# Side work of TensorE in a scan row: kv blocks, attention and projection issued at other states of a decoder kernel

## Chip, core and metric

One core of a Trainium2 chip. The metric is the device time of one execution in microseconds (us), as the median of several runs. The kernel before has a median of 1000.1 us of 3 runs (999.48 to 1000.89). All arithmetic is in f32.

## What is computed

A decoder layer on `x` of shape (4, 512, 512) with a context of shape (4, 512, 256). It has three stages, each with a residual and a normalization. The last stage (a feed-forward net whose weights are read from a table of 16 values by index) is not touched by the change.

```python
x = layernorm(x + attention(x, weight_qkv, weight_proj))      # 16 heads of 32, 4 kv heads, over the 4 positions
x = layernorm(x + ssm(ctx_1024, x, ...))                      # x is the gate
x = layernorm(x + ffn(x, lut, gate_idx, up_idx, down_idx))

# attention: seq is axis 0 of x (4 positions), batch is axis 1 (512)
scores = einsum("bhqd,bhkd->bhqk", q, k) / sqrt(32)           # causal over 4 positions
out = softmax(scores) @ v @ weight_proj.T

# ssm, for each of the 4 rows b of the context:
x  = einsum("ed,bld->bel", in_proj_w, hidden)                 # 512 channels, 512 steps
u  = silu(causal_conv(x, conv_w) + conv_b)
dt_lo, B, C = split(einsum("ke,bel->bkl", x_proj_w, u))       # 16, 16, 16
delta = softplus(dt_proj_w @ dt_lo + dt_proj_b)
state[n] = state[n] * exp(delta * A[n]) + delta * u * B[n]    # 16 states n, scan over the 512 steps
y = sum_n state[n] * C[n] + D * u
y = y * silu(z)
```

## The kernel before

**The scan.** The ssm is worked off in four rows b (0 to 3), one for each row of the context. A row has 16 states n, and a state has four units et, one for each block of 128 channels. A unit is one scan on VectorE over 512 steps (`scan`, line 1166). Before it TensorE transposes the scaled input of the unit into one of four PSUM banks (`input_transposed`, line 630, "input transposes" below), for which ScalarE has made `scaled` (line 865), and ScalarE makes the decay of the unit (line 876, a ring of eight). After the scan GpSimd multiplies the state with the repeated row of C (line 1414). When a state's four units are done, GpSimd issues a DMA that adds the whole state into `y_scratch` in DRAM (`add_group`, line 1425, 1 MB); the buffer of the state is free again when that has landed. There are four such buffers, so the scan of state n waits for the addition of state n-4 (`group_sum`). States with an odd n are added into a second tensor, and one DMA per row adds this to the first (`add_odd_sum`, line 1432, at state 4 of the next row). The last eight states of row 3 are summed on TensorE instead (`state_summed`, line 639).

**Order.** TensorE transposes for unit k once the scan of unit k-4 is done, so it runs at most four units ahead of VectorE. Every engine works in order. There is no planner: the tables that begin at line 174 say after which unit (n, et) of a row a job is issued, and the functions of each engine are written to agree with them.

**Side jobs.** While row b is scanned, TensorE also does the attention of position block b (`attention_transposed`, "att" i for positions i = 3, 0, 2, 1, line 583), its projection (`project`, line 592), and for the next row: the input projection (`in_proj`, line 519), x_proj (line 542), the kv blocks (`project_kv`, "kv" s, four of them, line 528), the transposes of B and u (lines 549, 561), dt (`delta_mm`, line 555), q (line 534), and the transposes of delta (line 568). These jobs use PSUM banks 4 to 7 in rotation, by their place in `ORDERED` (`BANK`): a job waits until the job four places before it has been read out (`freed`, `bank_freed`). Two of the places belong to "expneg", on which TensorE does nothing and which only takes a bank for ScalarE.

**Who reads them.** ScalarE copies att (`keep_attT`, line 845), kv (`keep_kv`, line 789), B and C (`keep_bc`, line 799), and does the first half of softplus (`softplus_parts`, lines 811 to 820), each at the end of a state n of its loop, behind the scaled inputs and the decays for state n+2. VectorE does the second half (`softplus`, lines 1128, 1131, 1133, 1138) after the units (9,0) and (11,0), and the head products of q after (11,2), (11,3) and (12,1). Its third step, line 1133, is the last to read the bank of dt (`base_ready`). VectorE adds the projection to x (`residual`, line 1153) and takes its statistics; GpSimd makes the normalization factors (`norm_factors`, lines 1437 to 1445), and ScalarE applies them (`normalized`, line 853).

**GpSimd in a row** does the four products of each state, ten products of the attention's weights with v in states 0 to 3 (`weighted_values`, line 1403), and issues the additions: that of state n after the product of unit (n+1, 1).

**Row 3** has no next row, so its attention, projection, residual and normalization come early in the row (`LAST_ATT_AT`, `LAST_PROJ_AT`, `LAST_RES_AT`). SP loads the finished rows 0 to 2 (`load_row`, lines 418 and 420, 768 KB and 1 MB) at states 8 to 10, each after the repeated C row of its state has been issued, which waits for the products of the state before.

## Time and profile before

| | |
|---|---|
| median of 3 runs | 1000.1 us |
| the profiled execution | 997.59 us, of it 995.8 us from the first to the last instruction |
| the scan of rows 0 to 3 | from 54.4 to 551.1 us of the span |
| TensorE, share of the span busy | 87% (864.1 us) |
| VectorE | 76% (757.6 us) |
| ScalarE | 68% (674.1 us) |
| GpSimd | 50% (495.0 us) |
| granted TensorE clock, mean | 0.909 of 2.4 GHz |

Times in the profile are microseconds from the start of the span, if not marked ns. PE is TensorE, PEld its weight loads, DVE VectorE, ACT ScalarE, POOL GpSimd, SP SyncE. L630 is line 630 of the kernel. A line of a timeline has the start, the duration, the engine, the line and the operation, how many were merged (x4), and in brackets the idle time of the engine before it and what ended that. The granted clock is a share of 2.4 GHz: 1.00 is 2.4 GHz and 0.50 is 1.2 GHz. The shares of the whole span say little about the scan, in which each stretch has another engine or the DMA that ends last; the waits and the timelines tell that.

### The profile page before, as it was taken

The page shows a single profiled execution, that of the slowest core. Times are in us where ns is not written, and L with a number is a line of the kernel's source. Part 1 is how long each engine was busy: PE and PEld are TensorE (multiplying, and loading weights), DVE is VectorE, ACT ScalarE, POOL GpSimd, SP SyncE. Part 2 cuts the span into 40 slices and gives each one's busy share as a digit, 9 for nine tenths or more (in the row PEclk, how much of TensorE's full clock was granted, in tenths as well). Part 3 has the DMA queues.
Part 4 walks back from the last instruction along what each step waited for, and adds up shares of the span by engine and source line. Part 5 has one row for each costly group of instructions (what it writes and reads, how often), then busy time and mean ns, then how long its engine had stood idle before and what let it go on. Part 6 is the DMA issues. An engine that isn't in the chain of part 4 may idle for free.

```text
span 995.8 us, 11868 instructions
## 1 busy us (share of the span) xinstructions
PE 864.1 (87%) x3824; PEld 624.7 (63%) x3824; DVE 757.6 (76%) x1053; ACT 674.1 (68%) x994; POOL 495.0 (50%) x458
## 2 busy tenths in 40 slices
PE   6879887797779778788878988899999999899997
PEld 3447544476445565446544566787777778688885
DVE  3797898875898859987678776888888888345542
ACT  4698985788956898659598365767777776242321
POOL 0079867897857979569999731122211221001000
PEclk9889788897679796997878989999999999999999
DMA  8167989589976799977999022111111110223211
GB/s 263 34 178 171 203 182 210 134 222 239 211 197 139 201 223 234 226 146 166 220 255 324 36 96 85 43 43 56 49 42 42 42 63 21 74 85 99 93 64 53
DMA packets 49907, 135.98 MB, mean 137 GB/s; under 512 B 5364, under 2 KB 13684, under 8 KB 41156
## 3 DMA queue, kind: packets, MB, share of 16 engines
q0 software_dynamic: 8064, 58.72, 30.5%
q1 hardware_dynamic: 40432, 76.44, 22.6%
q10 hardware_dynamic: 1364, 0.25, 0.2%
q8 instruction: 23, 0.38, 0.1%
q14 instruction: 24, 0.20, 0.1%
HBM read 57.93 MB, written 81.66 MB: 140 GB/s over the span
## 4 chain that ended last, share of the span: by engine, by line
PE 22%; issue 22%; DVE 14%; POOL 13%; DMA 9%; ACT 3%; DVEq 1%; ACTq 0%; POOLq 0%
DMA y_scratch<-state 9%; POOL state L1414 7%; PE banks L703 5%; PE banks L727 4%; PE banks L592 4%; DVE leaf L1194 3%; DVE w_gu L1194 3%; PE banks L630 3%; PE banks L639 3%; ACT leaf L984 2%; DVE state L1166 2%; PE banks L534 2%; POOL prod_a L1403 2%; POOL y_scratch L1425 1%; DVE idx_sb L1178 1%
## 5 line engine op out<-in xcount | busy, mean ns | idle before, releaser
L1414 POOL TENSOR_TENSOR state<-state,crep 128x512 f32<-128x512 f32 x256 | 350.7, 1658 | 67.5 <-DVE state L1166 67.5
L1166 DVE TENSOR_TENSOR_SCAN state<-decay,banks 128x512 f32<-128x512 f32 x256 | 296.5, 1204 | 73.8 <-PE banks L630 47.0
L703 PE MATMUL banks<-x2T,wgu 128*128 128x512 f32 x1056 | 246.5, 393 | 5.4 <-DVE hT L1244 4.0
L630 PE MATMUL banks<-ident,scaled 128*128 128x128 f32 x1024 | 175.5, 316 | 79.4 <-DVE state L1166 69.2
L630 PEld LDWEIGHTS banks<-ident,scaled 128*128 128x128 f32 x1024 | 138.2, 162 | 153.5 <-DVE state L1166 67.6
L703 PEld LDWEIGHTS banks<-x2T,wgu 128*128 128x128 f32 x1056 | 197.9, 189 | 52.9 <-DVE hT L1244 11.4
L876 ACT ACTIVATE decay<-delta,negA 128x512 f32<-128x512 f32 x256 | 171.0, 718 | 85.0 <-DVE state L1166 84.6
L865 ACT ACTIVATE scaled<-duT,BT 128x512 f32<-128x512 f32 x256 | 163.4, 716 | 0.0
L984 ACT ACTIVATE leaf<-idx_sb,table,table_gap 128x1024 f32<-128x1024 uint8 (+1 forms) x132 | 129.4, 1022 | 6.8 <-DVE w_down L1194 3.2
L1194 DVE COPY_PREDICATED leaf<-idx_sb,leaf 128x1024 f32<-128x1024 uint8 (+1 forms) x88 | 94.5, 1073 | 6.3 <-issue 5.5
L1497 POOL TENSOR_TENSOR pool_wait_here<-minus_half 128x1 f32<-128x1 f32 x22 | 4.3, 194 | 180.0 <-DVE w_gu L1194 115.4
L727 PE MATMUL banks<-x2T 128*128 128x512 f32 (+1 forms) x264 | 83.0, 396 | 3.5 <-DVE x2T L1353 3.5
L727 PE MATMUL banks<-x2T,wgu 128*128 128x512 f32 (+1 forms) x264 | 81.5, 390 | 0.0
L1537 POOL TENSOR_TENSOR rstd<-vareps,minus_half 128x1 f32<-128x1 f32 x16 | 8.7, 542 | 140.6 <-DVE vareps L1372 140.6
L1425 POOL DMA_DIRECT2D y_scratch<-state x52 | 59.2, 1139 | 14.4 <-DMA y_scratch<-state 14.4
L592 PE MATMUL banks<-wp,attT 128*128 128x512 f32 x128 | 61.4, 625 | 0.0
L727 PEld LDWEIGHTS banks<-x2T 128*128 128x128 f32 (+1 forms) x264 | 50.6, 192 | 14.6 <-issue 3.9
L727 PEld LDWEIGHTS banks<-x2T,wgu 128*128 128x128 f32 (+1 forms) x264 | 49.6, 188 | 10.4
L1194 DVE COPY_PREDICATED w_gu<-idx_sb,leaf 128x1024 f32<-128x1024 uint8 x33 | 53.3, 1615 | 3.0 <-issue 2.7
L1065 ACT ACTIVATE leaf<-leaf,shift,rstd 128x512 f32<-128x512 f32 x16 | 13.1, 816 | 62.6 <-DVE shift L1375 62.6
L534 PE MATMUL banks<-wqkv,xT_sb 128*128 128x512 f32 x96 | 47.7, 646 | 3.7 <-DVE conv_in L1133 3.7
L1077 DVE SCALAR_TENSOR_TENSOR conv_in<-banks,ch,conv_in 128x511 f32<-128x511 f32 (+2 forms) x48 | 35.4, 744 | 11.9 <-ACT conv_in L773 10.7
(137 smaller groups left out, 1125.0 us busy)
## 6 DMA issues: line engine op xcount, KB each, us to landing
y_scratch<-state POOLq DMA_DIRECT2D x52, 1024.0 KB, 8.8
crep<-c_scratch SPq DMA_DIRECT2D x64, 256.0 KB, 5.7
idx_sb<-in_idx SPq DMA_DIRECT2D x11, 512.0 KB, 3.5
xT_sb<-in_xT SPq DMA_DIRECT2D x16, 256.0 KB, 4.5
y_scratch<-u SPq DMA_DIRECT2D x4, 1024.0 KB, 6.0
y_scratch<-state SPq DMA_DIRECT2D x4, 1024.0 KB, 6.3
y_scratch<-y_scratch POOLq DMA_DIRECT2D x4, 1024.0 KB, 12.8
leaf<-x_scratch SPq DMA_DIRECT2D x16, 256.0 KB, 2.8
```

What stands on the lines that cost most here:

```text
L534: last = mm(banks[:, bank, :], xT_sb[:, t, s, :], wqkv[:, t, 0:QT * P], start=t == 0, stop=t == HT - 1)
L592: last = mm(banks[:, bank, :], attT[:, s, t if s else 0, :], wp[:, t, :], start=t == 0, stop=t == QT - 1)
L630: last = nc.tensor.transpose(banks[:, k % NB, lc * LQ:(lc + 1) * LQ], scaled[:, g % SR, lc, et * P:(et + 1) * P], ident[:])
L703: last = mm(banks[:, 2 * tb + w, :], wgu[par][:, w, ws, t * P:(t + 1) * P], x2T[:, tb, xs, t, :], start=t == 0 and n == 0, stop=t == HT - ...
L727: last = mm(banks[:, bank, :], h[0:rows], w[0:rows, f, :], start=f == 0 and n == 0, stop=f == FT - 1 and n == 2)
L865: A(scaled[:, g % SR, lc, :], duT[m % 2][:, lc, :], ACT.Copy, scale=BT[:, m % 2, lc, n:n + 1])\
L876: A(decay[:, k % DR_RING, :], delta[m % 2][:, et, :], ACT.Exp, scale=negA[:, et, n:n + 1])\
L984: A(buffer(LEAF_ROLE[j], kind, parity), bit_of(0, kind, parity), ACT.Identity, bias=table[:, 2 * j:2 * j + 1], scale=table_gap[:, j:j + 1] ...
L1166: V.tensor_tensor_scan(state[:, g % GR, et, :], decay[:, k % DR_RING, :], banks[:, k % NB, :], 0.0, ALU.mult, ALU.add).then_inc(scan_ready, 1)
L1194: V.copy_predicated(buffer(kept, kind, parity), bit_of(bit, kind, parity), buffer(other, kind, parity)).then_inc(mux_ready, 1)
L1414: G.tensor_tensor(state[:, g % GR, et, :], state[:, g % GR, et, :], crep[:, g % CR, :], ALU.mult)\
L1425: pool.dma_start(total[:, b], group(g), accum_op=ALU.add).then_inc(group_sum(g)[0], 16)
```

## The change

In rows 0 to 2, attention 2 is issued after unit (3,2) instead of (4,1), kv 0 and 1 after (5,0) and (5,2) instead of (4,2) and (4,3), kv 2 and 3 after (9,1) and (9,2) instead of (6,0) and (6,1). ScalarE's copies of them move to match: attention 2 from state 4 to 3, kv 0 and 1 from 4 to 5, kv 2 and 3 from 5 to 9, ahead of the softplus parts. As banks go by the order of jobs, the jobs that a job waits for change too.

In row 3, the four attention jobs, the four projections, the residual adds, the normalization and the copies go to later units, the row loads on SP from states 8 to 10 to states 9 to 11, and the loads of the lookup table and of the first indices from state 11 to 12.

```diff
-                   (4, 2): ("kv", 0), (4, 3): ("kv", 1), (6, 0): ("kv", 2), (6, 1): ("kv", 3),
+                   (5, 0): ("kv", 0), (5, 2): ("kv", 1), (9, 1): ("kv", 2), (9, 2): ("kv", 3),
...
-        ATT_AT = {(3, 0): 3, (3, 1): 0, (4, 1): 2, (6, 0): 1}
-        LAST_ATT_AT = {(3, 0): 3, (3, 1): 0, (4, 0): 2, (5, 0): 1}
+        ATT_AT = {(3, 0): 3, (3, 1): 0, (3, 2): 2, (6, 0): 1}
+        LAST_ATT_AT = {(3, 2): 3, (3, 3): 0, (4, 2): 2, (6, 0): 1}
...
-        LAST_PROJ_AT = {(5, 1): 3, (5, 3): 2, (6, 1): 1, (6, 3): 0}
+        LAST_PROJ_AT = {(6, 2): 3, (7, 0): 2, (7, 2): 1, (8, 0): 0}
...
-                        if b == S - 1 and n == 8:
+                        if b == S - 1 and n == 9:
                             sp.wait_ge(shift_ready, S)
                             sp.wait_ge(x1_out, 16 * (S - 1))
-                        if b == S - 1 and 8 <= n < 8 + S - 1:
-                            load_row(n - 8)
-                        if b == S - 1 and n == 11:
+                        if b == S - 1 and 9 <= n < 9 + S - 1:
+                            load_row(n - 9)
+                        if b == S - 1 and n == 12:
                             sp.dma_start(table[:], lut.to_broadcast([P, 16])).then_inc(lut_in, 16)
...
-                        if n == 2:
+                        if n == (2 if more else 3):
                             keep_attT(b, 3)
                             keep_attT(b, 0)
-                        elif n == (4 if more else 3):
+                        elif n == (3 if more else 4):
                             keep_attT(b, 2)
-                        elif n == (5 if more else 4):
+                        elif n == 5:
                             keep_attT(b, 1)
-                        if n == 8 and not more:
+                        if n == 9 and not more:
                             normalized(b)
...
                             elif n == 4:
                                 keep_bc(m)
+                            elif n == 5:
                                 keep_kv(c, 0)
                                 keep_kv(c, 1)
-                            elif n == 5:
-                                keep_kv(c, 2)
-                                keep_kv(c, 3)
                                 keep_bt(m)
...
                             elif n == 9:
+                                keep_kv(c, 2)
+                                keep_kv(c, 3)
                                 softplus_parts(m, (2, 3))
...
-                LAST_RES_AT = {(5, 2): 3, (6, 0): 2, (6, 2): 1, (7, 0): 0}
+                LAST_RES_AT = {(6, 3): 3, (7, 1): 2, (7, 3): 1, (8, 1): 0}
...
-                            if at == ((15, 2) if more else (7, 1)):
+                            if at == ((15, 2) if more else (8, 2)):
                                 norm_factors(b)
```

## Rows read from the trace of the kernel before

**Rows 1.** Waits of VectorE, 205 to 249 us: total us, times, longest.

```profile
DVE state L1166 <- PE banks L630: 8.4, 6, 3.1
```

**Rows 2.** Timeline of VectorE, rows 0 and 1: start, us, operation, idle before.

```profile
116.43 1.29 DVE L1128 TENSOR_SCALAR delta<-banks 128x512 f32<-128x512 f32 x2
...
237.25 4.55 DVE L1166 TENSOR_TENSOR_SCAN state<-decay,banks 128x512 f32<-128x512 f32 x4 [5.53 <-DMA y_scratch<-state]
...
251.92 1.28 DVE L1133 SCALAR_TENSOR_TENSOR conv_in<-banks,conv_in 128x512 f32<-128x512 f32 x2
...
254.31 8.99 DVE L1166 TENSOR_TENSOR_SCAN state<-decay,banks 128x512 f32<-128x512 f32 x8
```

**Rows 3.** Chain that ended last, row 1: start, us, what.

```profile
219.22 18.01 DMA y_scratch<-state
...
237.75 10.63 DMA y_scratch<-state
```

**Rows 4.** Stretches: length, busy PE, PEld, DVE, ACT, POOL; clock, DMA share, GB/s.

```profile
79.00:119.00 40.00, 34.62 (x202) 26.71 (x200) 30.48 (x30) 39.94 (x71) 39.17 (x34) 0.91 0.88 182
187.00:219.00 32.00, 23.36 (x141) 17.99 (x140) 26.83 (x28) 28.72 (x46) 32.00 (x30) 0.89 0.79 203
219.00:249.00 30.00, 24.02 (x136) 18.89 (x136) 19.03 (x17) 27.18 (x50) 24.29 (x23) 0.83 1.01 232
```

**Rows 5.** Waits of ScalarE, 79 to 118 us (row 0).

```profile
ACT decay L876 <- DVE state L1166: 0.4, 1, 0.4
```

**Rows 6.** Timeline of ScalarE, row 0: copies of kv 2 and 3, Ln.

```profile
101.40 0.67 ACT L789 ACTIVATE kv<-banks 128x256 f32<-128x256 f32 x2
...
115.80 1.09 ACT L820 ACTIVATE conv_in<-banks 128x512 f32<-128x512 f32 x2
```

**Rows 7.** Timeline of VectorE, row 3: states 7 and 11 to 15.

```profile
498.96 1.22 DVE L1166 TENSOR_TENSOR_SCAN state<-decay,banks 128x512 f32<-128x512 f32 x1 [1.59 <-DMA y_scratch<-state]
...
526.30 24.80 DVE L1166 TENSOR_TENSOR_SCAN state<-decay,banks 128x512 f32<-128x512 f32 x20 [6.95 <-DMA y_scratch<-state]
```

**Rows 8.** Timeline of GpSimd, row 3: normalization factors and the addition of state 7.

```profile
506.24 0.23 POOL L1437 TENSOR_SCALAR vareps<-meanvar 128x4 f32<-128x4 f32 x1
...
508.16 4.96 POOL L1414 TENSOR_TENSOR state<-state,crep 128x512 f32<-128x512 f32 x4
513.08 0.91 POOL L1425 DMA_DIRECT2D y_scratch<-state  x1
```

**Rows 9.** Chain that ended last, row 3.

```profile
513.08 13.20 DMA y_scratch<-state
```

**Rows 10.** DMA issues of the page: count, KB each, median us to landing.

```profile
y_scratch<-state POOLq DMA_DIRECT2D x52, 1024.0 KB, 8.8
```

**Rows 11.** Timeline of TensorE, row 1: a kv block, input transposes, dt 2.

```profile
224.31 1.89 PE L528 MATMUL banks<-wqkv,xT_sb 128*128 128x256 f32 x8
226.04 0.60 PE L630 MATMUL banks<-ident,scaled 128*128 128x128 f32 x4
...
252.65 2.07 PE L555 MATMUL banks<-bc_dt,dt_w 17*128 17x512 f32 x2 [2.10 <-DVE conv_in L1133]
```

**Rows 12.** Stretches again, columns as in rows 4.

```profile
252.10:262.20 10.10, 8.70 (x25) 5.29 (x26) 10.10 (x12) 9.11 (x17) 8.53 (x8) 0.50 1.04 229
...
525.20:531.90 6.70, 4.23 (x11) 2.67 (x12) 5.59 (x6) 3.76 (x6) 5.33 (x5) 0.50 1.03 407
```

**Rows 13.** Timeline of TensorE: q 3 of rows 0 and 1, q 2 of row 2.

```profile
133.24 5.05 PE L534 MATMUL banks<-wqkv,xT_sb 128*128 128x512 f32 x8 [0.31 <-DVE conv_in L1133]
...
266.32 6.76 PE L534 MATMUL banks<-wqkv,xT_sb 128*128 128x512 f32 x8 [1.70 <-DVE conv_in L1133]
...
403.71 3.60 PE L534 MATMUL banks<-wqkv,xT_sb 128*128 128x512 f32 x8
```

**Rows 14.** Timeline of SP, row 3: first row load.

```profile
511.12 0.42 SPq L418 DMA_DIRECT2D rows_in<-x_scratch  x1
```

**Rows 15.** Timeline of TensorE, row 3: input transposes of (12,0).

```profile
527.67 1.09 PE L630 MATMUL banks<-ident,scaled 128*128 128x128 f32 x4 [6.13 <-DVE state L1166]
```

## Prediction, made before the changed kernel was run

> **What bounds the kernel now.** I read the views in this order: who waited for whom on VectorE, the busy time of the engines by stretch, the chain that ended last, and then the timelines around each moved job. The scan takes 64 groups of four units ("state n of row b" below is one group; "(n, et)" is one unit); the change touches nothing outside it. The question for each moved job is whether TensorE is what ends last where it stands, and where it will stand.
>
> Row 1 stands for rows 1 and 2, which repeat each other. In its states 3 to 8 VectorE waits 8.4 us for the input transposes [rows 1], because attention, x_proj and the kv blocks stand before them in TensorE's queue. The reader is to see that a second wait comes behind these: the scan of state 7 starts at 237.25 after 5.53 us without work, released by a DMA [rows 2]. That DMA is the addition of state 3, issued at 219.22 and landed 18.01 us later [rows 3]. GpSimd issues it, and GpSimd is busy for 32.00 of the 32 us before that [rows 4]: ten attention products and four state products per state, with no wait for a scan. From 219 to 249 the 16 DMA engines are busy all the time (share 1.01), by the addition, the sum of the odd states and the repeated C rows [rows 4]. So here a faster TensorE moves neither the issue nor the landing. The next addition follows in the same chain (237.75, 10.63 us) [rows 3], and it releases state 9. After that VectorE has no gap up to the q jobs: softplus and scans are back to back [rows 2].
>
> Row 0 has no sum of a row before it, and additions land in time. But ScalarE is busy for 39.94 of the 40 us from 79 to 119 [rows 4], with one wait of 0.4 us [rows 5]: silu, decays, scaled inputs, evictions, softplus parts. Its last Ln starts at 115.80 [rows 6] and softplus on VectorE at 116.43 [rows 2], so ScalarE is what ends last there.
>
> In row 3 GpSimd and the DMA bound the first half as in row 1. The end is set by one wait: the scan of state 11 starts at 526.30 after 6.95 us of waiting [rows 7] for the addition of state 7, which GpSimd issued at 513.08 [rows 8] and which took 13.20 us [rows 9], where the median of 52 such additions is 8.8 [rows 10].
>
> **The change, part by part.** *States 3 to 6, rows 0 to 2.* Attention 2 goes from (4,1) to (3,2), kv 0 and 1 from (4,2), (4,3) to (5,0), (5,2), kv 2 and 3 from (6,0), (6,1) to (9,1), (9,2). The TensorE waits there (7.7 of the 8.4 us; the rest are in state 8) shrink to some 4 us. In rows 1 and 2 this is worth nothing: the cover is GpSimd's queue and the 18.01 us landing, and they don't move. In row 0 ScalarE is the cover, and the one thing taken from its queue before the softplus is the pair of evictions of kv 2 and 3, 0.67 us as a pair with an overlap of about 0.1 [rows 6]: -0.6 us. ScalarE's other evictions only change places, each behind a decay that waits for the scan of the same state, so the matmul it waits for is done by then: nothing.
>
> *kv 2 and 3 in state 9.* This is the term that costs. The banks of side jobs rotate over four, by the order of jobs. In the new order kv 2 takes the bank of dt 0 and kv 3 that of dt 1, which are free only when the third step of softplus (L1133) has read them. That step stands in VectorE's queue behind the scan (9,0) and starts at 251.92 [rows 2]; today dt 2 waits for the same thing and starts at 252.65 [rows 11]. So kv 2 starts at 252.65 with the transposes of (9,2), (9,3) and of state 10 queued behind it, which today are done at 249. VectorE gets to (9,1) at 254.31 [rows 2] and would want (9,2) at 255.45 and (9,3) at 256.58. TensorE has to do kv 2 (1.89 us as a span, 1.73 without its drain), transposes (0.44 of its 0.60), kv 3, transposes [rows 11]: 2 x 2.17 = 4.34 us at the full clock, ready at 256.99: 0.4 late. But the clock is granted at 0.50 (1.2 GHz) from 252.1 to 262.2 [rows 12], and dt 2 runs 2.07 us in it [rows 11]; the wait before kv 2 will be longer than today's, so I take this level for its start. How much a dense run begun just after such a fall loses until 2.4 GHz is back is bounded by the q jobs: 5.05 us in row 0 and 6.76 in row 1 against 3.60 at the full clock [rows 13]: 1.45 to 3.16 us lost. So (9,3) comes 1.9 to 3.6 us late; the middle is 2.75 us. dt 2 and 3 behind it fit between the scans (a wait of 0.86 for each against 1.13 for a scan). Nothing between here and the row's end can take it back, since VectorE is on the path. Three rows: 3 x 2.75 = +8.25 us; bounds 3 x 0.4 (full clock all through) and 3 x 3.6.
>
> The Trainium skill (TensorE: Matmul & The Clock Gate, section "Why this matters for your kernels") speaks against this change: it asks for matmuls kept together, since gaps bring the slow clock back, while spreading makes gaps. The rows agree in kind (0.50 after each idle stretch). What it makes of the time is the rival of the half clock that holds, below.
>
> *q jobs.* They begin 3 us later, and the clock may be at another level then. Today q 3 is at half clock in part in rows 0 and 1 and at the full one in row 2 [rows 13]. Row 1 could gain up to the 3.2 us, row 2 could lose as much. I take 0, with 3 us to both sides.
>
> *Row 3.* Attention and projection go back by 2 to 6 units, the residual adds too (to (6,3), (7,1), (7,3), (8,1)), the normalization factors on GpSimd from (7,1) to (8,2), the row loads on SP from state 8 to 9, the lookup table and the indices from 11 to 12. Up to the scan of state 7 (498.96, released by a DMA [rows 7]) the jobs have slack of GpSimd's making. Then there are three effects. (1) The factors take GpSimd 506.24 to 508.16 ahead of the products that precede the addition of state 7 [rows 8]. Behind it, that issue moves from 513.08 to 511.1. (2) The first row load, 1.77 MB, is issued at 511.12 [rows 14] and shares the DMA engines with the addition. At state 9 SP first waits for the products of state 8 (about 517), so the addition runs nearly alone: between the median of 8.8 and its own 13.20 [rows 9, 10] I take 11.2, landed at 522.3. (3) Against it: two residual adds (3.1 us of VectorE) now stand in state 7 and one in state 8, where one stood. The scans of states 9 and 10 go back, and state 11 can start at 521.6 to 522.8. Both ends meet at about 522.6: 3.7 us ahead of 526.30. (4) TensorE stands idle for 6.13 us before the next transposes at 527.67 and runs them and the first state sums at 0.50 clock up to 531.9 [rows 12, 15]; with the gap gone, half of its 4.23 busy us in that stretch, 2.1 us, can go too; I take 1.5. ScalarE's normalization now waits for the factors until 516 and ends at 519, ahead of the decays of state 12 that are wanted at 525. GpSimd's products, back to back at 4.9 us a state from 517, end at 552, before TensorE's last sum at 555.5: no new bound. The last row load moves only if the odd sum does, and is wanted 3 us later than it comes. Sum: -5.2 us; bounds -1.5 and -6.2.
>
> For the shared DMA engines the Trainium skill (Trainium Kernel Development and Optimization, section "Key Constraints") says that DMAs from SP, ScalarE and GpSimd run on the same 16 engines and interleave. The trace agrees: 13.20 against 8.8 us. If the queues were apart, effect (2) would be nothing and the gain of row 3 some 3 us.
>
> Sum: -0.6 + 8.25 - 5.2 = **+2.4 us**. It is made against the profiled execution (span 995.8, its own time 997.59) and put on the median of 1000.1, which lies 2.5 us above that execution and more than 1 us above no run shown: 1002.5.
>
> **The rivals.**
> *The clock comes back early (faster).* If TensorE is at 2.4 GHz when kv 2 starts, or is so within a microsecond, the cost is 0.4 to 1 us a row, and with row 3 at -5.8 the sum is -0.6 + 1.5 - 5.8 = -4.9: 995.2. It turns at 1.7 us a row. For it: row 1's clock is 1.00 just before 252, and today's run there is not dense. Against: both q runs, and the idle stretch before kv 2 grows.
> *Row 3 gives nothing.* The row load only meets the addition at another moment, or VectorE's later residuals set state 11: +7.6, less 1.5: 1006 to 1008.
> *The half clock holds.* 3.6 us in all three rows, +10.8 - 0.6 - 5.2 = +5.0: 1005.
> *The TensorE waits were the bound.* Then 3 x 4 us go and row 3's too: about -14, 986. Against it speaks the release of state 7 by a DMA in rows 1 to 3.
> *The change does not take effect*: excluded for the order of jobs; all tables are read by all engines.
>
> **How the numbers follow.** Forecast (0 to +5 us) 0.52, early clock 0.18, row 3 gives nothing 0.14, half clock holds 0.11, TensorE the bound 0.05. The range takes in the early clock's -4 and row 3's loss up to +7: 996.0 to 1007.0. What measurement can tell from no change is 0.2%, 2 us. The forecast's case lies around that bound: of its 0.52, 0.25 fall within and 0.27 above. Faster 0.22 (0.17 early clock, 0.05 TensorE the bound), within 0.2% 0.27, slower 0.51 (0.27 + 0.13 + 0.11).
>
> **What would show it.** State 7 of rows 1 and 2 should start as long after the first scan of its row as now, with a longer wait for the DMA; TensorE's kv 2 should start with L1133 of VectorE as its releaser; VectorE should have new waits for transposes at (9,2), (9,3), 2 to 3.6 us a row; state 0 of row 3 should start 5 to 10 us late; the addition of state 7 in row 3 should take under 12 us and the wait before state 11 shrink to about nothing. The prediction is wrong if state 9 shows no wait (clock at 1.00), or if row 3 from state 0 to the last sum isn't 4 to 6 us shorter.

## The result and the profile after

| | before | after |
|---|---|---|
| median, runs | 1000.07 us, 6 | 1008.25 us, 6 |
| lowest to highest | 999.48 to 1002.00 | 1005.09 to 1009.93 |
| the profiled execution | 997.59 us, span 995.8 | 1006.42 us, span 1004.6 |

The ratio is 1.0084 (95% interval 1.0067 to 1.0102): 8.2 us slower, where +2.4 was forecast, and above the range. First where the profiled execution became longer. The times are those of scans and of GpSimd's products, read from the timelines of both traces.

| stretch of the span | before | after | difference |
|---|---|---|---|
| start to the first scan | 54.43 | 55.45 | +1.0 |
| row 0, first scan to first scan of the next row | 127.50 | 128.69 | +1.2 |
| row 1 | 133.96 | 136.04 | +2.1 |
| row 2 | 130.03 | 136.44 | +6.4 |
| row 3, first scan to end of the last scan | 105.19 | 98.84 | -6.4 |
| row 3, first scan to end of TensorE's last state sum (L639) | 115.09 | 108.74 | -6.4 |
| row 3, first scan to end of GpSimd's last product (L1414) | 107.16 | 105.68 | -1.5 |
| GpSimd's last product to the end of the span | 442.70 | 442.27 | -0.4 |

In these two executions rows 0 to 2 cost 9.7 us; by the other traces of this study it is 7.3 to 9.3 (worked out under "Why the prediction was wrong"). Row 3 gave the scans and TensorE's sums even more than forecast (6.4 for 5.2). But the span became shorter by 1.5 + 0.4 there: it followed GpSimd, not TensorE. 1.0 + 9.7 - 1.5 - 0.4 = 8.8.

**Rows 0 to 2.** The timeline of VectorE after, row 0 and then row 1, answers [rows 2]:

```profile
116.89 1.29 DVE L1128 TENSOR_SCALAR delta<-banks 128x512 f32<-128x512 f32 x2 [1.52 <-ACT conv_in L820]
...
124.63 1.22 DVE L1166 TENSOR_TENSOR_SCAN state<-decay,banks 128x512 f32<-128x512 f32 x1 [1.74 <-PE banks L630]
126.79 3.44 DVE L1166 TENSOR_TENSOR_SCAN state<-decay,banks 128x512 f32<-128x512 f32 x3 [0.94 <-PE banks L630]
...
239.19 4.55 DVE L1166 TENSOR_TENSOR_SCAN state<-decay,banks 128x512 f32<-128x512 f32 x4 [10.18 <-DMA y_scratch<-state]
...
253.84 1.28 DVE L1133 SCALAR_TENSOR_TENSOR conv_in<-banks,conv_in 128x512 f32<-128x512 f32 x2
...
258.48 1.22 DVE L1166 TENSOR_TENSOR_SCAN state<-decay,banks 128x512 f32<-128x512 f32 x1 [1.04 <-PE banks L630]
260.64 3.44 DVE L1166 TENSOR_TENSOR_SCAN state<-decay,banks 128x512 f32<-128x512 f32 x3 [0.94 <-PE banks L630]
```

State 7 of row 1 starts 239.19 - 184.15 = 55.0 us after the row's first scan, where it was 55.3 (237.25 - 181.93), with 10.18 us of waiting for the DMA instead of 5.53: what TensorE gave back in states 3 to 6 went into that wait, and nothing else. In its place there are two new waits for TensorE at (9,2) and (9,3), 2.68, 1.98 and 2.14 us in rows 0, 1, 2. TensorE's side of them, with what ended its pause ([rows 11] show a kv block of 1.89 us):

```profile
120.02 3.78 PE L528 MATMUL banks<-wqkv,xT_sb 128*128 128x256 f32 x8 [5.66 <-DVE conv_in L1133]
...
254.57 3.43 PE L528 MATMUL banks<-wqkv,xT_sb 128*128 128x256 f32 x8 [4.27 <-DVE conv_in L1133]
...
258.27 1.89 PE L528 MATMUL banks<-wqkv,xT_sb 128*128 128x256 f32 x8
```

kv 2 waits for the third step of softplus, runs at 1.2 GHz after a pause of 4.3 to 5.7 us (granted clock 0.50 during it in row 0, 0.57 in row 1) and takes 3.4 to 3.8 us; kv 3 is at 2.4 GHz again (1.00 in row 1). This execution was a mild one. In kv23_only (below), and in the same way in four more traces with the pair in state 9, rows 1 and 2 lost more: kv 2 took 3.78 us and kv 3 still 2.1 to 2.7. Row 1 of kv23_only, where the granted clock was 0.50 during kv 2 and 0.77 during kv 3:

```profile
254.00 3.78 PE L528 MATMUL banks<-wqkv,xT_sb 128*128 128x256 f32 x8 [4.41 <-DVE conv_in L1133]
257.58 1.06 PE L630 MATMUL banks<-ident,scaled 128*128 128x128 f32 x4
258.43 2.46 PE L528 MATMUL banks<-wqkv,xT_sb 128*128 128x256 f32 x8
```

The waits of state 9 add up to 8.5 to 9.5 us over the three rows in these five traces, where the profiled execution of the changed kernel has 6.8.

**Row 3.** GpSimd's timeline answers [rows 8], and the DMA view of the microsecond of its issue (size, median us from issue to landing) answers [rows 9]:

```profile
520.99 1.46 POOL L1425 DMA_DIRECT2D y_scratch<-state  x1
522.09 1.67 POOL L1414 TENSOR_TENSOR state<-state,crep 128x512 f32<-128x512 f32 x1
523.85 0.23 POOL L1437 TENSOR_SCALAR vareps<-meanvar 128x4 f32<-128x4 f32 x1
```
```profile
y_scratch<-state POOLq DMA_DIRECT2D x1, 1024.0 KB, 10.0
```

The addition of state 7 is issued ahead of the factors and lands in 10.0 us instead of 13.20. VectorE's timeline then shows the 30 scans from (8,2) on in one piece, where [rows 7] had 6.95 us of waiting, and behind them the line that the forecast had not looked at:

```profile
520.79 34.68 DVE L1166 TENSOR_TENSOR_SCAN state<-decay,banks 128x512 f32<-128x512 f32 x30
555.39 6.96 DVE L1305 TENSOR_TENSOR table_gap<-table 128x8 f32<-128x8 f32 x1
562.38 0.17 DVE L1307 TENSOR_SCALAR table_gap<-table_gap 128x8 f32<-128x8 f32 x1
562.46 2.29 DVE L1210 TENSOR_TENSOR rows_in<-rows_in,gate_in 128x2048 f32<-128x2048 f32 x1
564.67 1.29 DVE L1173 TENSOR_SCALAR idx_sb<-idx_sb 128x1024 int32<-128x1024 int32 x2
...
573.30 4.42 DVE L1225 TENSOR_SCALAR vareps<-meanvar 128x2 f32<-128x2 f32 x1
```

A subtraction of 128x8 values lasts 6.96 us, and it ends with GpSimd's last product (562.31). In the kernel before it lasted 2.08 us and ended with that product too (553.08). VectorE there, and GpSimd's second gate product:

```profile
551.03 2.08 DVE L1305 TENSOR_TENSOR table_gap<-table 128x8 f32<-128x8 f32 x1
...
568.93 0.17 DVE L1225 TENSOR_SCALAR vareps<-meanvar 128x2 f32<-128x2 f32 x1
```
```profile
563.90 4.52 POOL L1481 TENSOR_TENSOR rows_in<-rows_in,gate_in 128x2048 f32<-128x2048 f32 x1
```

GpSimd after, from its last products on:

```profile
552.37 9.94 POOL L1414 TENSOR_TENSOR state<-state,crep 128x512 f32<-128x512 f32 x8
567.29 4.57 POOL L1481 TENSOR_TENSOR rows_in<-rows_in,gate_in 128x2048 f32<-128x2048 f32 x1 [4.98 <-issue]
...
573.16 4.53 POOL L1481 TENSOR_TENSOR rows_in<-rows_in,gate_in 128x2048 f32<-128x2048 f32 x1
577.79 1.74 POOL L1488 TENSOR_TENSOR rstd<-vareps,minus_half 128x2 f32<-128x2 f32 x1
```

So behind GpSimd's last product hangs a chain of fixed length: table_gap, a gate product on VectorE, the index bits (four in two pairs), two gate products on GpSimd, then the norm's power, which is queued behind them. Before, the second gate product ended at 568.42, 0.7 us before the norm's tensor_scalar, which comes by way of TensorE, was done (568.93 + 0.17); TensorE just set the end. After, the same tensor_scalar could start at 573.30, and the norm waits for GpSimd until 577.7.

### The profile page after: what moved, and what is told of

It is laid out like the page before. It is cut to its first block, busy times and chain, and to the rows that moved or that the text cites. A ratio compares the mean times of both kernels' runs of the same rounds, so it can differ in the third digit from the quotient of the medians.

```text
span 1004.6 us, 11868 instructions
## 1 busy us (share of the span) xinstructions
PE 861.9 (86%) x3824; PEld 623.5 (62%) x3824; DVE 765.5 (76%) x1053; ACT 674.7 (67%) x994; POOL 494.9 (49%) x458
## 4 chain that ended last, share of the span: by engine, by line
issue 19%; PE 16%; DVE 11%; ACT 3%; POOL 3%; DMA 2%; DVEq 0%; ACTq 0%; POOLq 0%
PE banks L703 5%; PE banks L727 4%; DVE leaf L1194 3%; PE banks L639 3%; DVE w_gu L1194 3%; DMA y_scratch<-state 2%; ACT leaf L984 2%; POOL state L1414 2%; PE banks L630 1%; PE banks L592 1%; DVE state L1166 1%; DVE idx_sb L1178 1%; DVE w_down L1194 1%; PE banks L676 1%; POOL rstd L1537 1%
## 5 line engine op out<-in xcount | busy, mean ns | idle before, releaser
L1414 POOL TENSOR_TENSOR state<-state,crep 128x512 f32<-128x512 f32 x256 | 351.9, 1700 | 75.9 <-DVE state L1166 75.8
L630 PE MATMUL banks<-ident,scaled 128*128 128x128 f32 x1024 | 168.6, 305 | 72.0 <-DVE state L1166 64.1
L630 PEld LDWEIGHTS banks<-ident,scaled 128*128 128x128 f32 x1024 | 131.4, 156 | 138.6 <-DVE state L1166 57.8
L1425 POOL DMA_DIRECT2D y_scratch<-state x52 | 62.8, 1207 | 14.4 <-DMA y_scratch<-state 14.4
L592 PE MATMUL banks<-wp,attT 128*128 128x512 f32 x128 | 66.5, 669 | 0.0
L1065 ACT ACTIVATE leaf<-leaf,shift,rstd 128x512 f32<-128x512 f32 x16 | 13.1, 816 | 62.6 <-DVE shift L1375 62.6
L528 PE MATMUL banks<-wqkv,xT_sb 128*128 128x256 f32 x128 | 37.0, 444 | 14.4 <-DVE conv_in L1133 14.4
```

The source lines that it names most:

```text
L592: last = mm(banks[:, bank, :], attT[:, s, t if s else 0, :], wp[:, t, :], start=t == 0, stop=t == QT - 1)
L630: last = nc.tensor.transpose(banks[:, k % NB, lc * LQ:(lc + 1) * LQ], scaled[:, g % SR, lc, et * P:(et + 1) * P], ident[:])
L1414: G.tensor_tensor(state[:, g % GR, et, :], state[:, g % GR, et, :], crep[:, g % CR, :], ALU.mult)\
L1425: pool.dma_start(total[:, b], group(g), accum_op=ALU.add).then_inc(group_sum(g)[0], 16)
```

## The experiments

The theories were made after the result was known. Theory A: the loss of rows 0 to 2 is all kv 2 and 3 in state 9. Theory C: the row-3 moves free TensorE by 6 us, but GpSimd's products set the end, so that they are worth 1 to 2 us. Theory B: the many gaps lower TensorE's clock everywhere.

**Parts of the change.** Four kernels. kv23_back is the changed kernel with:

```diff
-(9, 1): ("kv", 2), (9, 2): ("kv", 3)      # NEXT_AT
+(6, 0): ("kv", 2), (6, 1): ("kv", 3)
 # and keep_kv(c, 2), keep_kv(c, 3) in state 5 instead of 9
```

> The changed kernel with kv 2 and 3 put back after (6,0) and (6,1), their ScalarE copies in state 5; all else as changed. Theory A (kv 2 and 3 wait in state 9 for the banks of dt 0 and 1 and hold up the transposes; that is the whole loss of rows 0 to 2): no wait of VectorE for transposes in state 9, each row 0 to 2 some 2.5 us shorter than in the changed kernel, the total 7 to 10 us below it, at 998 to 1001. Theory B (the gaps that spreading makes keep TensorE at 1.2 GHz in more places, q and projection above all): half of the loss stays, 1003 to 1006.

kv23_only is the kernel before with only that pair moved, the other way:

```diff
-(6, 0): ("kv", 2), (6, 1): ("kv", 3)
+(9, 1): ("kv", 2), (9, 2): ("kv", 3)
```

> The kernel before with kv 2 and 3 alone moved to (9,1) and (9,2), copies in state 9. Theory A: slower than before by 6 to 10 us (rows 0 to 2 together 8 to 10 longer), 1006 to 1010. Theory B: only part of it, 1002 to 1005.

row3_only is the kernel before with LAST_ATT_AT, LAST_PROJ_AT, LAST_RES_AT, the factors, the loads and the evictions of row 3 as in the change; rows012_only is the changed kernel with all of these as before:

```diff
-LAST_PROJ_AT = {(5, 1): 3, (5, 3): 2, (6, 1): 1, (6, 3): 0}
+LAST_PROJ_AT = {(6, 2): 3, (7, 0): 2, (7, 2): 1, (8, 0): 0}
...
-if b == S - 1 and 8 <= n < 8 + S - 1:
+if b == S - 1 and 9 <= n < 9 + S - 1:
```

> The kernel before with the moves of row 3 alone (attention, projection, residual, normalization, row loads, table and index loads). Theory C (after the last scan the first VectorE operation with two SBUF inputs can't run until GpSimd has finished its last product, and the chain from there sets the end; TensorE's earlier end is worth nothing): scans of row 3 end 4 to 6 us earlier, GpSimd's last product 1 to 2 us earlier, the total 1 to 2 us below before, 998 to 999.5. The sum of the prediction (TensorE's last sum is the end): 5 us below, 995.

> The changed kernel with row 3 as before. Theory A with C: all of the loss and none of the 1 to 2 us of row 3: 1008 to 1011. By the prediction's sum for row 3: 1013.

Measured, beside runs of the kernel before on the same chip (median 999.51):

| kernel | median (lowest to highest) | ratio to before, 95% interval |
|---|---|---|
| kv23_back | 1000.03 (995.70 to 1001.91) | 1.0004 (0.9991 to 1.0016) |
| kv23_only | 1008.29 (1007.99 to 1011.34) | 1.0096 (1.0076 to 1.0116) |
| row3_only | 997.63 (994.22 to 999.99) | 0.9980 (0.9967 to 0.9993) |
| rows012_only | 1009.42 (1008.38 to 1010.55) | 1.0099 (1.0078 to 1.0121) |

Theory A holds within the intervals: the pair alone costs 9.6 us, and taking it back gives 8.0 (1.0084 - 1.0004). The row-3 moves are worth 2.0 us on the kernel before and 1.5 on the changed one (1.0099 - 1.0084), not 5.2: theory C. Theory B falls: with all moves but the pair in place the time is that of before. row3_only came 0.4 us under the 998 to 999.5 expected of it. The other moves of states 3 to 6 lie between +0.3 (rows012_only less kv23_only) and +2.4 us (kv23_back less row3_only), too near the intervals to tell. kv23_back isn't free of side effects: its row 0 took 77.3 us up to state 11, where the kernel before took 74.6, so the 8.0 is a less clean price of the pair than the 9.6.

The profiles of the four say which engine the end follows (us of each span, from the timelines):

| kernel | first scan to last scan's end, row 3 | last state sum to the end | GpSimd's last product to the end |
|---|---|---|---|
| before | 105.2 | 434.8 | 442.7 |
| kv23_only | 104.8 | 434.9 | 443.2 |
| rows012_only | 104.8 | 435.0 | 443.3 |
| after | 98.8 | 439.2 | 442.3 |
| kv23_back | 98.6 | 439.2 | 442.2 |
| row3_only | 98.8 | 439.1 | 442.1 |

From the first scan of row 3 to the end of the span it is 549.6 to 549.9 us in the three with row 3 as before, and 547.7 to 548.0 in the three with row 3 moved: 1.6 to 2.2 us, as the medians have it. (The execution of row3_only that was profiled was the slowest of its 11, 999.99 us; its row 3 is what is read here.)

With row 3 as before, TensorE's last sum and GpSimd's last product are both as far from the end as they can be, and neither has more than 1.2 us to spare. With row 3 moved, TensorE's sum comes 4.3 us earlier than the end can use, and the distance from GpSimd stays.

**The clock at kv 2.** Is it the clock that makes the two blocks cost 2 to 2.7 us a row, or their place behind the bank? The changed kernel, with matmuls of no use in the pause of TensorE (their output is overwritten):

```diff
 pe.wait_ge(*((scan_ready, k - NB + 1) if k >= NB else ramp_freed(k)))
+if g < DS * (S - 1) and g % DS == 9 and et == 1:
+    for _ in range(3):            # 5 in warm_kv5
+        mm(banks[:, k % NB, :], ident[:], wqkv[:, 0, 0:512], start=True, stop=True)
```

> Edit: the changed kernel, with three 128x512 matmuls of no use (into the bank that the next input transposes overwrite) ahead of the transposes of place (9,1) of rows 0 to 2, so that TensorE's matmuls come closer together before kv block 2. Clock theory (the kv blocks cost 2.0 to 2.7 us each row in state 9 because they run at 1.2 GHz): the clock is up when kv block 2 starts, the two blocks take half as long, the idle time of VectorE until TensorE in state 9 falls from 2.68, 1.98, 2.14 us to under 1 each, and the time comes to 1003 to 1006. Bank theory (the wait is the kv blocks' place in the ring of banks, at either clock): the waits of state 9 stay at 2 us or grow by the length of the added matmuls, and the time is 1008 to 1012.

> Edit: as warm_kv, with five idle-time matmuls instead of three. In warm_kv the pause of TensorE before kv block 2 was 4.22, 2.38 and 2.13 us in rows 0 to 2, the first kv block took 3.78, 2.54 and 1.99 us, and VectorE waited 2.88, 2.22 and 0.66 us in state 9: where the block was fast, the wait was short. Clock theory: the pauses are under 2.5 us in all rows, the kv block takes 2.0 to 2.6 us, the waits of state 9 are 0.4 to 1.2 us each and the time is 1000.5 to 1003. Rival (row 2 was chance, or the added matmuls delay the transposes of (9,1)): the waits stay at 2 us, the time is 1003 to 1007.

Measured: warm_kv 1003.16 us, ratio 1.0039 (1.0019 to 1.0059); warm_kv5 1003.28, ratio 1.0033 (1.0016 to 1.0049); the changed kernel had 1.0084. The execution of warm_kv that was profiled was the slowest of its 12, 1006.25 us, so its trace shows waits but not the gain. kv 2 on TensorE in warm_kv5, rows 0, 1 and 2:

```profile
119.10 3.65 PE L528 MATMUL banks<-wqkv,xT_sb 128*128 128x256 f32 x8 [2.67 <-DVE conv_in L1136]
...
255.49 1.89 PE L528 MATMUL banks<-wqkv,xT_sb 128*128 128x256 f32 x8
...
389.69 1.99 PE L528 MATMUL banks<-wqkv,xT_sb 128*128 128x256 f32 x8
```

| VectorE waits for TensorE in state 9, rows 0, 1, 2 | kv 2 takes | the waits |
|---|---|---|
| after | 3.78, 3.43, 3.59 | 2.68, 1.98, 2.14 |
| warm_kv | 3.78, 2.54, 1.99 | 2.88, 2.22, 0.66 |
| warm_kv5 | 3.65, 1.89, 1.99 | 2.24, 1.21, 0.66 |

Where kv 2 ran at 2.4 GHz behind a short pause the wait was 0.66 us, and where it ran at 1.2 GHz 2 us and more. Row 1 fits least: in warm_kv kv 2 took 2.54 us and the wait did not shrink, since kv 3 behind it took 2.65 us and VectorE waited 1.65 us for that one; and in warm_kv5 1.21 us were left at the full clock, since the five matmuls took 6.08 us and kept TensorE until 255.49, 0.9 us after softplus's step (from 253.99, 0.64 for each half) had freed the bank. Row 0 stayed at 1.2 GHz in both, after pauses of 4.22 and 2.67 us, so the expectation for it was missed. Against the profiled execution of the changed kernel the waits of state 9 fell by 6.80 - 4.11 = 2.7 us in warm_kv5, and the span by 2.9 (1001.7); against the five other traces with the pair in state 9 they fell by 4.3 to 5.4 us, which is what the medians have (some 5 us, 1.0084 - 1.0033). The time of warm_kv5 lies just above the 1000.5 to 1003 of the clock theory and inside the rival's range, and five matmuls gained no more than three; so the times don't decide, and the traces carry the reading: the clock sets most of the size of the waits in rows 1 and 2, row 0 stays unanswered, and the bank sets that there are waits at all.

**What bounds the end of row 3.** The changed kernel with work of no use added, on one engine each:

```diff
 # pool_plus2, GpSimd
+if not more and at in ((10, 0), (10, 2)):
+    G.tensor_tensor(delta0[:, 2 + et // 2, :], delta0[:, 0, :], delta0[:, 1, :], ALU.mult)
 output_product(k)
 # pe_plus4, TensorE
+for et in range(ET):
+    mm(banks[:, 0, :], ident[:], state[:, (DS * S - 1) % GR, et, :], start=True, stop=True)
 rest_summed()
```

> Edit: the changed kernel, with two more GpSimd products (128x512, data of no use) in state 10 of row 3. Theory C (since the change GpSimd's last product, at 562.3 in the trace, sets the end by way of table_gap, the row products and the norm): all of the 2.4 to 2.9 us that the two take come through, the time is 1010.5 to 1011.5. Rival (TensorE's last sum of states still sets the end, as it did before the change): GpSimd's products have slack, and the time stays within 1 us of the changed kernel's, at 1008 to 1009.

> Edit: the changed kernel, with four more 128x512 matmuls on TensorE right ahead of its last sums of states (some 0.85 us each at 1.2 GHz as the trace has it, 3.4 us in all at that clock, half of it at 2.4). Theory C (GpSimd's chain ends last by 8.8 us of what TensorE's path gave before, TensorE's own path has about 3 us of slack): the time moves by less than 0.7 us, to 1008 to 1009. Rival (TensorE's last sum sets the end): 1.7 to 3.4 us slower, 1010 to 1012.

Measured: pe_plus4 1007.59 us, ratio 1.0086 (1.0059 to 1.0113). The four matmuls took the 3.4 us, at a granted clock of 1.00 (the expectation had put their 0.85 us each down to 1.2 GHz; it is their time at 2.4), and the norm's sum still waited for the gate product of GpSimd:

```profile
564.97 3.60 PE L662 MATMUL banks<-state,ident 128*128 128x512 f32 x8
```
```profile
576.49 1.10 DVE L1227 TENSOR_SCALAR vareps<-meanvar 128x2 f32<-128x2 f32 x1
```
```profile
573.05 4.51 POOL L1483 TENSOR_TENSOR rows_in<-rows_in,gate_in 128x2048 f32<-128x2048 f32 x1
```

(VectorE and then GpSimd.) It cost nothing that can be told, against +3.4 if TensorE had set the end: from the first scan of row 3 to the end of the span it is 548.6 us, as in warm_kv and warm_kv5, whose row 3 is untouched, and 548.0 in the changed kernel. The rival falls. pool_plus2 took 1009.67 us, ratio 1.0104 (1.0078 to 1.0131): 1.4 to 2 us over the changed kernel and between the two expectations, so that the times alone don't decide. Its trace has the two products at 1.28 us each and the end of the last one 2.4 us later from the row's first scan (108.09 for 105.68). From row 3's first scan to the end of the span it is 549.6 us, 1.0 to 1.6 more than in these. So a good part of the 2.4 us came through, but not all of it, as theory C has it. The gate product and the norm's power follow back to back on GpSimd:

```profile
556.75 8.92 DVE L1305 TENSOR_TENSOR table_gap<-table 128x8 f32<-128x8 f32 x1 [0.40 <-DMA table<-in_lut]
```
```profile
578.73 4.50 POOL L1483 TENSOR_TENSOR rows_in<-rows_in,gate_in 128x2048 f32<-128x2048 f32 x1
583.19 0.72 POOL L1490 TENSOR_TENSOR rstd<-vareps,minus_half 128x2 f32<-128x2 f32 x1
```

**Why 128x8 take 7 us.** The changed kernel with four tiny instructions of no use between the scans of row 3:

```diff
 scan(UN * b + ET * n + et)
+if not more and at in ((12, 2), (13, 2)):
+    V.tensor_reduce(stats[:, n - 12, 0:1], minus_half[:], AX.X, ALU.add)
+if not more and at in ((13, 0), (14, 0)):
+    V.tensor_tensor(stats[:, n - 11, 0:4], minus_half[:], minus_half[:], ALU.add)
```

> Edit: the changed kernel, with four tiny VectorE instructions of no use between the scans of row 3, all on data long in SBUF: at (12,2) and (13,2) a tensor_reduce with one SBUF input (128x4 to 128x1), at (13,0) and (14,0) a tensor_tensor with two SBUF inputs (128x4). Lock theory (a VectorE instruction with two SBUF inputs can't run beside GpSimd's products and waits out a whole stretch of them, and shows that as its own duration): each tensor_tensor lasts 4 to 10 us, until GpSimd has no further scan to multiply, each tensor_reduce 0.1 to 0.3 us. Rival (the 6.96 us of the table_gap instruction after the change are a wait for its table, or something of that place alone): all four last 0.1 to 0.3 us.

VectorE's timeline, and then GpSimd's beside it:

```profile
542.04 0.13 DVE L1283 TENSOR_REDUCE stats<-minus_half 128x1 f32<-128x4 f32 x1
542.09 2.32 DVE L1166 TENSOR_TENSOR_SCAN state<-decay,banks 128x512 f32<-128x512 f32 x2
544.32 6.95 DVE L1285 TENSOR_TENSOR stats<-minus_half 128x4 f32<-128x4 f32 x1
...
553.44 0.12 DVE L1283 TENSOR_REDUCE stats<-minus_half 128x1 f32<-128x4 f32 x1
...
555.72 0.51 DVE L1285 TENSOR_TENSOR stats<-minus_half 128x4 f32<-128x4 f32 x1
...
563.95 0.95 DVE L1309 TENSOR_TENSOR table_gap<-table 128x8 f32<-128x8 f32 x1
564.93 1.19 DVE L1311 TENSOR_SCALAR table_gap<-table_gap 128x8 f32<-128x8 f32 x1
```
```profile
544.87 6.38 POOL L1418 TENSOR_TENSOR state<-state,crep 128x512 f32<-128x512 f32 x5
552.48 13.62 POOL L1418 TENSOR_TENSOR state<-state,crep 128x512 f32<-128x512 f32 x11 [1.24 <-DVE state L1166]
```

The first tensor_tensor lasts 6.95 us: until GpSimd has done all five products it had scans for (544.87 + 6.38 = 551.25) and stands idle. The two tensor_reduces, each beside a product, last 0.13 and 0.12 us. The second tensor_tensor lasts 0.51, short of the 4 us expected of it. The first had used up GpSimd's backlog: by now only one product was running, and VectorE waited until that one ended (556.21). table_gap at the end of the same trace lasted 0.95 us: it ended with the running product (564.87), though one more was to come, whose scan had ended at 564.03; the tensor_scalar behind it then waited for that one (566.10). In the 13 other traces the first VectorE instruction behind the scans, whose wait this is, waited out every product that was left, two to eight of them. Why it was let in between two here is open. The rival, that only table_gap's own place or table is slow, falls: these data were long in SBUF. One run, 1012.8 us.

The Trainium skill (SBUF — State Buffer, section "Who interferes with whom") says that a VectorE instruction with two SBUF inputs contends with a GpSimd instruction that reads SBUF, that a tensor_scalar can too, and that a tensor_reduce doesn't. The traces agree in all three kinds. It says that whichever of the two starts first holds the pair of ports for one instruction. Here the loser waited through five products back to back, and by the profile's records it had started, at 544.32, in a stretch without a product (544.24 to 544.87, GpSimd issuing a DMA); how that fits isn't shown.

**Moving what stands behind the lock.** On the kernel before and on row3_only, the gate product of row 1 goes from GpSimd to VectorE; on row3_only alone, the index bits go ahead of table_gap:

```diff
 # row3_gate, before_gate
-ON_POOL = {1: 1, 2: 2}
-GATED = {0: 1, 3: 5}
+ON_POOL = {2: 1}
+GATED = {0: 1, 1: 2, 3: 6}
 gate_y(0)
+gate_y(1)
 # bits_first
+spread_bits(*FIRST); spread_bits(*SECOND); single_bits(*FIRST); single_bits(*SECOND)
 dve.wait_ge(lut_in, 16)
```

> Edit: the kernel before with the row-3 moves alone (row3_only, 997.6), and the gate product of row 1 (4.55 us on GpSimd behind the index bits) given to VectorE (2.3 us, ahead of the index bits). Theory C (with row 3 moved, the end goes by VectorE's table_gap, GpSimd's gate products and the norm that waits for them): GpSimd's chain loses 4.55 and starts 2.3 later, so 1.5 to 2.5 us faster than row3_only, 995 to 996. Rival (TensorE's last sums set the end): the gate product on VectorE goes ahead of the last row's gate product and costs up to 2.3 us, 998 to 1000.

> Edit: the kernel before with the same gate product given to VectorE. Theory C: in the kernel before, GpSimd's second gate product ended at 568.42, 0.5 us ahead of the norm that waits for TensorE's sums, so there is only that to gain and the added 2.3 us of VectorE end at 560.2, ahead of TensorE's last sums (561.0): the time stays within 1 us of before, 999 to 1001. Rival (GpSimd's chain set the end in the kernel before too): 2 us faster, 998.

> Edit: row3_only, with the four index-bit instructions of VectorE (tensor_scalar, one SBUF input, 1.29 us a pair) put ahead of table_gap's subtraction. If an instruction with one SBUF input runs beside GpSimd's products, they are done in the 7.0 us in which the subtraction now waits, GpSimd's first gate product starts 2.5 us earlier, and the time is 1.5 to 2.5 us below row3_only's 997.6. If such a tensor_scalar is held up as well (the norm's tensor_scalar lasted 4.4 us under GpSimd's gate product), its duration is 5 to 7 us, and the time stays at 997 to 998.

Measured, beside a median of 1000.31 of the kernel before: row3_gate 997.10 us, ratio 0.9974 (0.9957 to 0.9990); before_gate 1000.32, ratio 1.0004 (0.9987 to 1.0021); bits_first 997.71, ratio 0.9980 (0.9960 to 1.0000).

before_gate came as theory C has it, with nothing to gain. row3_gate missed its 995 to 996 by a microsecond. In its trace the norm's tensor_scalar was free 13.1 us after GpSimd's last product (567.3 - 554.19), where row3_only had 15.4, so the 2.3 us are there; but the distance to the end of the span fell by only 1.1 (442.1 to 441.0), and the intervals of the two kernels overlap. Both are faster than the kernel before and the changed one; which of the two is faster is open.

bits_first says what else is held up. Its VectorE:

```profile
547.81 8.06 DVE L1173 TENSOR_SCALAR idx_sb<-idx_sb 128x1024 int32<-128x1024 int32 x2
555.80 1.28 DVE L1178 TENSOR_SCALAR idx_sb<-idx_sb 128x1024 int32<-128x1024 int32 x2
557.00 0.15 DVE L1309 TENSOR_TENSOR table_gap<-table 128x8 f32<-128x8 f32 x1
```

The pair of tensor_scalars, 1.29 us elsewhere, now lasts 8.06 and waits for the same product (554.71), and table_gap, with GpSimd idle, lasts 0.15. Whatever stands first behind the scans pays; the time stays.

## Why the prediction was wrong

By the steps of its sum, in the profiled executions. For the step of the q jobs, TensorE's timeline after, q 3 of rows 0, 1 and 2:

```profile
136.97 3.70 PE L534 MATMUL banks<-wqkv,xT_sb 128*128 128x512 f32 x8 [1.29 <-DVE conv_in L1133]
...
270.82 5.40 PE L534 MATMUL banks<-wqkv,xT_sb 128*128 128x512 f32 x8 [1.30 <-DVE conv_in L1133]
...
407.19 5.40 PE L534 MATMUL banks<-wqkv,xT_sb 128*128 128x512 f32 x8 [1.30 <-DVE conv_in L1133]
```

- **States 3 to 6, rows 1 and 2, nothing**: right. State 7 starts 55.0 and 55.2 us into the row, where it was 55.3 and 54.8.
- **Row 0, -0.6**: right. Softplus starts 61.4 us into the row (116.89 - 55.45), and 62.0 before (116.43 - 54.43).
- **kv 2 and 3 in state 9, +8.25**: right in mechanism, and near in size in these two executions. The waits for TensorE in state 9 add up to 6.8 us, and from the first scan to state 11 the rows grew by 2.7, 2.3 and 3.2 us, 8.2 in all for the +7.65 of this step and the one above. The pair alone measured 9.6 us by the medians, and 8.0 taken back. The releaser is L1133 as forecast, and kv 2 runs at 1.2 GHz. At the full clock 0.66 us were left, where the working had 0.4. The other traces put the term higher. Up to state 11, rows 0 to 2 took 233.9 to 234.4 us in the five traces without the pair in state 9 and with the other moves of these rows undone, and 244.0 to 244.8 in the five traces beside the profiled one that have it (kv23_only, rows012_only, pe_plus4, pool_plus2, port_probe): 9.6 to 10.9 us for 7.65, near the 3.6 a row of the rival "the half clock holds", since kv 3 ran partly at 1.2 GHz too.
- **q jobs, 0 with 3 us to both sides**: state 11 became -1.4, -1.4 and +1.7 us longer in rows 0, 1, 2, -1.0 in all, as the clock of q 3 went (lines above; [rows 13] had 5.05 and 6.76 in rows 0 and 1). State 14, with the projection, became -0.2, +1.2 and +1.6 us longer, 2.6 in all. 8.2 - 1.0 + 2.6 give the 9.7 but for rounding. These two terms belong to the two executions and not to the change. In the same five traces against four without the pair (before_gate, row3_only, row3_gate, bits_first), state 11 took 53.6 to 54.3 us over the three rows against 51.7 to 52.2, and state 14 took 30.8 to 31.1 against 34.6 to 35.3: it became shorter, by 3.5 to 4.5. The working had no term for state 14 at all, and it paid back what kv 2 and 3 cost more than forecast.
- **The scans and sums of row 3, -5.2**: the mechanism was right, each link of it: issue ahead of the factors, 10.0 us for 11.2 taken, the wait before state 11 gone. It was a little more, -6.4 up to TensorE's last sum.
- **"GpSimd's products ... end at 552, before TensorE's last sum at 555.5: no new bound"**: this is the step that failed. The working's own numbers had GpSimd's last product move by only 1.1 us (552 for 553.08). It asked whether the products end before the last sum. It should have asked what hangs behind each of the two. Behind GpSimd's last product hang 442 us to the end, and behind TensorE's last sum 435; the product needs to be done some 7.4 us ahead of the sum (442.2 - 434.8), not just ahead of it. Before they were 7.9 apart (561.01 - 553.08), so both were bounds within a microsecond, and the tie was to be seen in the trace of before: GpSimd's gate product ending at 568.42 next to the norm's tensor_scalar at 568.93. Of the 6.4 us of row 3, 1.9 came through. That is 3.3 us of the forecast's error.

In the two profiled executions the errors add up: row 3 -1.9 for -5.2 (+3.3), rows 0 to 2 +9.7 for +7.65 (+2.1), the ramp, which the change doesn't touch, +1.0: 6.4 us, as 8.8 less 2.4. Of these only the first is shown by experiments (row3_only, pe_plus4, and the distances to the end of six kernels). The 1.0 and most of the 2.1 come from which executions were profiled. The one of the kernel before had short rows 0 to 2: 391.5 us, where the four others with the same rows have 393.8 to 394.7; the five others with the pair in state 9 have 402.0 to 403.1. By these, rows 0 to 2 cost 7.3 to 9.3 us, for 7.65 forecast, and with the 1.9 of row 3 the change costs 5.4 to 7.4; the medians have 8.2, with an interval from 6.7 to 10.2. The first scan lay between 54.4 and 56.1 us in all traces. So of the error of 5.8 us (8.2 for 2.4) row 3 is 3.3, and for the rest no single term is shown; that kv 2 and 3 and state 14 came near to the forecast in sum was luck, since neither did by itself.

Of the rivals, "row 3 gives nothing" came nearest with 1006 to 1008, but for another reason: the row loads did no harm. "The clock comes back early" would have been the gain of warm_kv5. The test that the prediction gave itself, row 3 shorter by 4 to 6 us up to the last sum, was met while the time was missed: it measured the engine that had stopped being the bound.

## What to carry to other kernels

When a stretch is shortened for one engine, put down for every engine that works behind it how far its last instruction is from the end of the span, not which of them ends last: two engines that end 8 us apart can both be the bound. A job moved to where its buffer comes free late runs behind a pause, at TensorE's lower clock, and everything in its queue pays: place it where the engine is busy just before. Don't place a small VectorE instruction with two SBUF inputs, or a tensor_scalar, where GpSimd has a backlog: it can last as long as the backlog.

## What the runs showed of the hardware

A VectorE tensor_tensor of 128x8 with both inputs in SBUF lasted 0.15 us with GpSimd idle, 2.08 us when the last two of GpSimd's products (1.2 us from one to the next) were left, one of them running, and 6.96 us when six were; a tensor_scalar on 128x2 went from 0.17 to 4.42 us beside a gate product of GpSimd. In all traces but one VectorE did not get in between two of the products; in port_probe it did, with one product left. The profile books this as the duration of VectorE's instruction, as busy time and with no wait, so that neither the view of the waits nor an idle time shows it. A scan, which reads one of its inputs from the banks, was not held up: 30 of them ran at 1.16 us each beside the same products (34.68 us). It works the other way as well. In bits_first GpSimd's first gate product, 4.55 us elsewhere, began just after a VectorE gate product of 2.29 us and lasted 6.54:

```profile
557.27 2.29 DVE L1210 TENSOR_TENSOR rows_in<-rows_in,gate_in 128x2048 f32<-128x2048 f32 x1
```
```profile
557.44 6.54 POOL L1481 TENSOR_TENSOR rows_in<-rows_in,gate_in 128x2048 f32<-128x2048 f32 x1 [2.72 <-DVE table_gap L1311]
```
